# A two-layer adapter network on one core: the order of work inside a step, and who issues the gathers

## The reference, cut to what matters

```python
def layer(x, A, B, ids, W, b, experts_A, experts_B, router):
    c = einsum('bni,bri->bnr', x, B[ids])        # rank-16 coefficients
    v = einsum('bnr,bor->bno', c, A[ids])        # back to 1024 features
    y = v @ W.T + b                              # dense part
    z = einsum('bth,erh->bter', v, experts_A)    # 4 experts of rank 8
    alpha = softmax(v @ router.T (+ bias, log prior in layer 0))
    return x + y + 2 * sum_e alpha_e * (z_e @ experts_B_e.T)
```

## Time and profile before

| | us |
|---|---|
| median of 3 runs | 335.08 (334.63 to 335.91) |
| the profiled execution: its own time | 334.41 |
| the profiled execution: its span | 332.7 |
| PE busy in the span | 307.0 (92%) |
| DVE, ACT, POOL busy | 220.1, 186.4, 63.3 |
| from the issue of a load of x to its landing, median of 28 | 5.0 |

### The profile page before, as it was taken

How to read it: one execution, slowest core, us unless ns; L and a number is a source line. 1 busy time by engine, 2 the same in 40 slices (tenths; PEclk the granted TensorE clock), 3 DMA queues, 4 the chain that set the end, 5 groups by cost and what they waited for, 6 DMA issues and landing times.

```text
span 332.7 us, 6476 instructions
## 1 busy us (share of the span) xinstructions
PE 307.0 (92%) x2048; PEld 284.4 (85%) x2048; DVE 220.1 (66%) x476; ACT 186.4 (56%) x384; POOL 63.3 (19%) x58
## 2 busy tenths in 40 slices
PE   5994998799989998999979999999999999999894
PEld 4453998589978998999979999999999999899783
DVE  2156887686738766686658666777668676864556
ACT  1446976946546565755466465646575657461520
POOL 5600000620042103320143003320332024200000
PEclk9999899999999999999999999999999999999999
DMA  7999973006870388126840587037811783041006
GB/s 267 345 365 381 347 208 156 0 8 167 300 224 0 104 243 302 51 60 212 286 139 0 158 284 250 2 103 244 299 47 55 255 292 92 0 193 62 1 0 252
DMA packets 30773, 56.16 MB, mean 169 GB/s; under 512 B 3633, under 2 KB 20050, under 8 KB 30754
## 3 DMA queue, kind: packets, MB, share of 16 engines
q1 hardware_dynamic: 29666, 52.97, 48.3%
q0 software_dynamic: 1088, 2.97, 2.5%
HBM read 39.15 MB, written 16.78 MB: 168 GB/s over the span
## 4 chain that ended last, share of the span: by engine, by line
issue 41%; PE 20%; DMA 13%; POOL 12%; DVE 6%; ACT 3%; SPq 2%; POOLq 1%; DVEq 0%; ACTq 0%
POOL xs_lo L952 8%; DMA out<-xraw 6%; DMA xraw<-x_in 6%; PE ps_d L307 3%; PE ps_d L309 3%; PE ps_d L308 3%; POOL a1s_lo L952 2%; DVE xs_lo L740 2%; DVE xraw L942 2%; PE ps_d L545 1%; PE ps_p L307 1%; PE ps_d L547 1%; ACT res L574 1%; SPq L253 1%; SPq L251 1%
## 5 line engine op out<-in xcount | busy, mean ns | idle before, releaser
L952 POOL TENSOR_TENSOR xs_lo<-xraw,xs_hi 128x512 fp32r<-128x512 f32 x28 | 36.0, 1290 | 182.5 <-ACT xs_hi L574 182.4
L307 PE MATMUL ps_d<-w1s_hi,a1s_hi 128*128 128x384 f32 (+1 forms) x192 | 63.9, 333 | 0.0
L309 PE MATMUL ps_d<-w1s_hi,a1s_lo 128*128 128x384 f32 (+1 forms) x192 | 62.0, 323 | 0.0
L308 PE MATMUL ps_d<-w1s_lo,a1s_hi 128*128 128x384 f32 (+1 forms) x192 | 61.9, 322 | 0.0
L942 DVE SCALAR_TENSOR_TENSOR xraw<-ps_d,lp,xraw 128x512 f32<-128x512 f32 x60 | 43.6, 748 | 22.5 <-PE ps_d L547 22.5
L574 ACT ACTIVATE xs_hi<-xraw 128x512 fp32r<-128x512 f32 x60 | 36.0, 626 | 26.4 <-DMA xraw<-x_in 25.9
L307 PE MATMUL ps_p<-xs_hi,bst_hi 128*128 128x256 f32 x120 | 36.5, 304 | 6.2 <-DVE bst_lo L740 2.4
L308 PEld LDWEIGHTS ps_d<-w1s_lo,a1s_hi 128*128 128x128 f32 x192 | 36.2, 189 | 0.0
L307 PEld LDWEIGHTS ps_d<-w1s_hi,a1s_hi 128*128 128x128 f32 x192 | 36.1, 188 | 0.0
L309 PEld LDWEIGHTS ps_d<-w1s_hi,a1s_lo 128*128 128x128 f32 x192 | 36.1, 188 | 0.0
L308 PE MATMUL ps_p<-xs_lo,bst_hi 128*128 128x256 f32 x120 | 34.5, 288 | 0.0
(11 more groups left out here) (227 smaller groups left out, 702.9 us busy)
## 6 DMA issues: line engine op xcount, KB each, us to landing
out<-xraw SPq DMA_DIRECT2D x31, 512.0 KB, 3.5
xraw<-x_in SPq DMA_DIRECT2D x28, 512.0 KB, 5.0
w_plain<-w SPq DMA_DIRECT2D x16, 512.0 KB, 8.9
abraw<-ab_tab SPq DMA_DIRECT2D x64, 128.0 KB, 2.1
b0raw<-b_tab SPq DMA_DIRECT2D x64, 64.0 KB, 2.0
xraw<-x_in POOLq DMA_DIRECT2D x4, 512.0 KB, 11.0
a_plain<-a SPq DMA_DIRECT2D x1, 512.0 KB, 3.6
out<-xraw SPq DMA_DIRECT2D x2, 256.0 KB, 2.7
```

The costliest lines, as they stand in the source:

```text
L307: pe.matmul(acc, lh, rh, start=first, stop=False, skip_group_check=True)
L308: pe.matmul(acc, lh, rl, start=False, stop=False, skip_group_check=True)
L309: return pe.matmul(acc, ll, rh, start=False, stop=final, skip_group_check=True)
L952: return pool.tensor_tensor(dst, whole, high.bitcast(F32), ALU.subtract)
```

## The change

Four edits. PE's order within a step: `wide(0)` is cut behind its third chunk, so that `route(0)` comes earlier, and `wide(2)` as a whole stands behind `query()`. ACT and DVE do the softmax and the coefficients of layer 0 first, and the takings of `wide(0)` and the b parts of the next step behind them; two chunks of `split_x` that stood before the exponential go behind the b parts too. DVE's low parts `ht` and `he` go into the softmax, before its wait for the exponential. POOL issues the 16 gathers of a step instead of SP, with the ids read into registers at the head of its step.

```diff
--- before.py
+++ after.py
@@ -244,7 +244,7 @@
 
                 return tuple(zip(values(g * GROUP, GROUP, ADAPT0), values(g * GROUP + SEQS, GROUP, SEQS)))
 
-            def gather(picks, seqs, signal=gathered):
+            def gather(picks, seqs, signal):
 
                 for b in seqs:
                     n0, n1 = picks[b]
@@ -263,20 +263,12 @@
             gather(picks, range(HSEQ, GROUP), first_gathered[1])
             for k in range(KT):
                 sp.dma_start(w1raw[k], w1[k]).then_inc(w1_in[k], 16)
-            picks = pick(1)
-            sp.wait_ge(b_lo, 4)
-            sp.wait_ge(a_lo, 1)
-            gather(picks, range(GROUP))
             sp.wait_ge(x_used, 2 * CH)
             for i in range(CH):
                 load_x(1, 1, i)
 
             def body(g, par, last):
                 ahead = not (isinstance(g, int) and g >= STEPS - 2)
-                if ahead:
-                    picks = pick(g + 2)
-                    sp.wait_ge(a_lo, g + 2)
-                    gather(picks, range(GROUP))
                 for i in range(CH - 1 if last else CH):
                     sp.wait_ge(d_out, KT * g + KC * (i + 1))
                     sp.dma_start(out[bass.ds(g, 1), :, KC * i:KC * (i + 1), :]
@@ -458,7 +450,7 @@
                             pick_m0(k - 3, (ps_s, ps_z)[k - 3])
                 else:
                     after_step(pe, d_out, KT * g)
-                    wide(0)
+                    wide(0, range(3))
 
                 pe.wait_ge(h_sum, 2 * g + 2)
                 if first:
@@ -470,9 +462,11 @@
                 pe.wait_ge(c0_lo, g + 1)
                 after_step(pe, l_done, 2 * g)
                 route(0, f0x)
-                if not first:
-                    wide(1)
-                wide(2, range(KT // 2))
+                if first:
+                    wide(2, range(KT // 2))
+                else:
+                    wide(0, range(3, KT))
+                    wide(1, range(2))
                 pe.wait_ge(ht_lo, g + 1)
                 for n in range(2):
                     mm = pe.matmul(ps_h[:, n * P:(n + 1) * P], pick[:], ht[:, n, :], start=True, stop=True,
@@ -480,7 +474,10 @@
                 mm.then_inc(htx_done, 1)
                 pe.wait_ge(l_done, 2 * g + 1)
                 turn()
-                wide(2, range(KT // 2, 3 * KT // 4 if last else KT))
+                if first:
+                    wide(2, range(KT // 2, KT))
+                else:
+                    wide(1, range(2, KT))
 
                 def query():
 
@@ -496,8 +493,8 @@
                               skip_group_check=True).then_inc(q_done, 1)
 
                 query()
-                if last:
-                    wide(2, range(3 * KT // 4, KT))
+                if not first:
+                    wide(2)
                 if first:
                     pick_m0(2, ps_h)
                 banks = result_banks(last)
@@ -523,14 +520,14 @@
                 if first:
                     pick_m0(3, ps_s)
                 if last:
-                    start_results((0, 1, 2, 3, 4))
+                    start_results((0, 1, 2, 3))
                 else:
                     project(g + 1, 1)
                 pe.wait_ge(l_done, 2 * g + 2)
                 turn()
                 if last:
-                    from_layers(5)
-                    from_layers(6)
+                    for m in (4, 5, 6):
+                        from_layers(m)
                 else:
                     if first:
                         pe.wait_ge(m0x_ready, 8)
@@ -661,10 +658,6 @@
 
             def body(g, par, last):
                 first = isinstance(g, int) and g == 0
-                if not last and not first:
-                    act.wait_ge(h_done, g + 1)
-                    split_b(g + 1)
-
                 def wide_high(n):
                     cols, at = WIDE_PARTS[n]
                     width = min(cols.stop, D) - cols.start
@@ -685,28 +678,21 @@
                     act.wait_ge(sm_step, 9 * g + 4 * layer + 3)
                     act.activation(ex[:], lg[:], ACT.Exp).then_inc(exp_done, 1)
 
-                wide_high(0)
                 act.wait_ge(ht_done, g + 1)
                 copy(ht[:, 0, :], ps_t[:, 0:P]).then_inc(ht_hi, 1)
                 copy(he[0:LR, :], ps_t[0:LR, P:2 * P]).then_inc(ht_hi, 1)
-                if not last and not first:
-                    split_x(g + 1, 1 - par, 0, [0, 1])
                 softmax_exp(0)
-                wide_high(1)
                 act.wait_ge(htx_done, g + 1)
                 for half in range(2):
                     copy(htx[L0ROWS[half], half, :, :].rearrange("p a n -> p (a n)"), ps_h[L0ROWS[half], 0:2 * P]
                          ).then_inc(htx_ready, 1)
                 coef_high(0)
-                if first:
-                    split_b(g + 1, QUARTERS[0:2])
+                wide_high(0)
                 if not last:
-                    split_x(g + 1, 1 - par, 0, range(CH) if first else [2, 3])
-                wide_high(2)
-                if first:
-                    split_b(g + 1, QUARTERS[2:4])
+                    split_b(g + 1, QUARTERS[0:2] if first else QUARTERS)
                 if not last:
-                    split_x(g + 1, 1 - par, 1, [0])
+                    split_x(g + 1, 1 - par, 0)
+                wide_high(1)
                 act.wait_ge(c1_done, 2 * g + 1)
                 for half in range(2):
                     cols = slice(half * HALF, (half + 1) * HALF)
@@ -715,8 +701,11 @@
                     copy(cf[L1ROWS[half], 0, cols], cm[L1ROWS[half], cols]).then_inc(c1_hi, 1)
                 if first:
                     m0x_high(0, 2, ps_h)
+                wide_high(2)
+                if first:
+                    split_b(g + 1, QUARTERS[2:4])
                 if not last:
-                    split_x(g + 1, 1 - par, 1, range(1, CH))
+                    split_x(g + 1, 1 - par, 1)
                 softmax_exp(1)
                 if first:
                     m0x_high(0, 3, ps_s)
@@ -881,6 +867,10 @@
                     dve.tensor_tensor(lg[:], logits,
                                       mx.rearrange("p (j a) -> p j a", a=1).to_broadcast([P, TT, EXP]),
                                       ALU.subtract).then_inc(sm_step, 1)
+                    if layer == 0:
+                        dve.wait_ge(ht_hi, 2 * g + 2)
+                        low(ht[:, 1, :], ps_t[:, 0:P], ht[:, 0, :])
+                        low(he[ELO, :], ps_t[0:LR, P:2 * P], he[0:LR, :]).then_inc(ht_lo, 1)
                     if layer == 1 and not last:
                         split_second_x(g + 1, 1 - par, [3])
                     dve.wait_ge(exp_done, 2 * g + layer + 1)
@@ -899,15 +889,11 @@
                                       lg[:].rearrange("p j (e a) -> p j e a", a=1)
                                       .to_broadcast([P, TT, EXP, ER]), ALU.mult).then_inc(l_done, 1)
 
+                softmax(0)
+                coef_low(0)
+                if not last:
+                    split_b(g + 1, (0, 1) if first else range(4))
                 wide_low(0)
-                dve.wait_ge(ht_hi, 2 * g + 2)
-                low(ht[:, 1, :], ps_t[:, 0:P], ht[:, 0, :])
-                low(he[ELO, :], ps_t[0:LR, P:2 * P], he[0:LR, :]).then_inc(ht_lo, 1)
-                softmax(0)
-                wide_low(1)
-                coef_low(0)
-                if first:
-                    split_b(g + 1, (0, 1))
 
                 dve.wait_ge(q_done, g + 1)
                 for half in range(2):
@@ -922,6 +908,7 @@
                     dve.wait_ge(c1_hi, 2 * g + half + 1)
                     low(cf[L1ROWS[half], 1, cols], cm[L1ROWS[half], cols], cf[L1ROWS[half], 0, cols]
                         ).then_inc(c1_lo, 1)
+                wide_low(1)
                 if first:
                     split_b(g + 1, (2, 3))
                 if not last:
@@ -984,12 +971,39 @@
                 pool.dma_start(xraw[0][:, KC * i:KC * (i + 1), :], x_in[0, :, KC * i:KC * (i + 1), :]
                                ).then_inc(x0_in[i], 16)
 
+            def values(first, count, limit):
+
+                return nc.values_load_multi_w_load_instructions(
+                    ids[0:1, bass.ds(first, count)], (mybir.EngineType.Pool,), min_val=0, max_val=limit - 1)[1]
+
+            def pick(g):
+
+                return values(g * GROUP, GROUP, ADAPT0), values(g * GROUP + SEQS, GROUP, SEQS)
+
+            def gather(n0s, n1s):
+
+                for b, (n0, n1) in enumerate(zip(n0s, n1s)):
+                    pool.dma_start(b0raw[:, b, :],
+                                   b0_tab[bass.ds(n0, 1)].rearrange("a p n -> p (a n)")).then_inc(gathered, 16)
+                    pool.dma_start(abraw[:, b, :, :].rearrange("p a n -> p (a n)"),
+                                   ab1_tab[bass.ds(n1, 1)].rearrange("a p n -> p (a n)")).then_inc(gathered, 16)
+
             def body(g, par, last):
+                ahead = not (isinstance(g, int) and g >= STEPS - 2)
+                if ahead:
```

(12 more changed lines are left out.)

## The result

The changed kernel takes 337.48 us (median of 18 runs, 336.36 to 339.76), the kernel before 334.99 beside it: the ratio is 1.0091, 95% interval 1.0067 to 1.0116. It is slower by 0.9%, where 333.8 us, 0.4% less and no measurable change, was forecast; 337.48 lies in the range of 330.5 to 338.5, but on the other side of the kernel before.

A forecast was written before the change was run, and what follows sets the result against it. PE, busy 92% at full clock, bounds the kernel, so only its waits can change. Six steps -0.4, first step +1.2, last -2.1: -1.3 on the 332.7 us span, median 333.8 us, range 330.5 to 338.5.

The forecast's parts named there:

- Gathers to POOL: SP loses 9 us of issuing, x lands by T + 10 (T: first ps_h matmul); POOL's issues cost nothing.
- Layer 0 first: In each middle step lp is ready at T + 7.55, before turn() at T + 8.27; 6.2 us of waits go.
- b parts and x behind the coefficients: POOL starts x at T + 14.25, ends at 19.35; PE gets a new wait of 0.8 us in project.
- chunks of over 1.3 us: Sign of being wrong: POOL's chunks of x's low parts taking over 1.3 us, against 1.27 to 1.29 assumed.
- The layer-1 coefficients: Before route(1), DVE's second cf low part waits for POOL, then f1s: route(1) at about T + 20.45, step 25.35 us.
- cost POOL nothing: Claim that POOL's start on x in the first step, with DVE still at a b part, cost POOL nothing.
- The start at 58.50: POOL's start on x's low parts in the first step before the change, taken as evidence that overlap costs POOL nothing.
- The sum: Whole span: -0.4 for six steps, +1.2 first, -2.1 last, together -1.3 us; 333.1 profiled, 333.8 median.
- the lock goes both ways: Rival: POOL also stands during DVE's low parts, PE's last chunk 0.75 us later, 5 us in all, 339; chance 0.14.
- Step 0: First step: POOL starts 0.4 us later, route(1) 0.8, project(1, 1) 1.2; +1.2 us, near 31.0.
- The last step: Final step: PE's 2.1 us wait for layer-1 coefficients goes, a 0.3 softmax wait may come; together -2.1 us.
- a real gain: Rival: POOL's pace and DVE's order don't bind, route(1) at 19.5, steps 24.35; about 328 us, halfway 331; chance 0.34.

The follow-up runs named there:

- e1: Kernel before with only the 16 gathers of a step issued by POOL instead of SP, other order unchanged: 356.46 us, ratio 1.0557 to the kernel before.
- e9: Changed kernel, whole work, layer-1 coefficients kept in PSUM so DVE's subtraction for cf's low part has one SBUF input: 329.72 us, ratio 0.9876 to the kernel before.
- e13: Changed kernel with extra matmuls nobody reads ahead of chunks 2 and 3 of project(g+1, 0), from step 1 on: 336.78 us, ratio 1.0045 to the kernel before.
- e14: e9 with the first step alone in the order of before on ACT and DVE: 327.89 us, ratio 0.9782 to the kernel before.
- e4: Changed kernel, POOL subtracting only the first half of each chunk of x's low part, work left out: 327.63 us, ratio 0.975 to the kernel before.
- e5: Changed kernel with DVE writing zeros instead of subtracting for the layer-1 coefficients' low part: 327.88 us, ratio 0.9784 to the kernel before.
- e6: Changed kernel with ACT, from step 1 on, taking x chunks before and between the b parts, wide(0) behind: 359.98 us, ratio 1.0744 to the kernel before.
- e2: Changed kernel with its gathers given back to SP, so the new order alone: 341.31 us, ratio 1.0176 to the kernel before.

## Why the prediction went wrong, by its own steps

**Gathers to POOL: right, but its cover was the order.** The issues take 0.54 us and end at T + 0.2; ACT's wait for x falls from 25.9 to 3.1 us. What I had not priced is the landing (2.1 to 4.0 us in the median); the new order hides it, and e1 shows the 5.6% it costs without.

**Layer 0 first: right.** turn() starts at T + 8.34 (8.27 forecast), with no wait for lp.

**b parts and x behind the coefficients: the place right, the pace off.** POOL starts at T + 14.31 (14.25) and ends at T + 19.74 instead of 19.35. Its four chunks take 5.43 us instead of 5.1. The prediction had named chunks of over 1.3 us as a sign of being wrong; the next paragraph says where they come from.

**The layer-1 coefficients: the step that failed.** The prediction let DVE wait for POOL, and put the price for POOL at nothing ("cost POOL nothing"). The lock goes both ways. In step 2, one chunk at a time:

```profile
134.74 0.69 DVE L729 TENSOR_TENSOR bst_lo<-abraw,bst_hi 128x512 fp32r<-128x512 f32 x1
135.06 1.51 POOL L939 TENSOR_TENSOR xs_lo<-xraw,xs_hi 128x512 fp32r<-128x512 f32 x1 [14.09 <-ACT xs_hi L571]
...
136.54 1.30 POOL L939 TENSOR_TENSOR xs_lo<-xraw,xs_hi 128x512 fp32r<-128x512 f32 x1
...
139.03 1.46 POOL L939 TENSOR_TENSOR xs_lo<-xraw,xs_hi 128x512 fp32r<-128x512 f32 x1
```

The first chunk starts while DVE is still at the last low part of b, and the last has cf's low parts beside it; with the third, at 1.28, the two between them keep the forecast pace. In e9, where the collision with cf is gone, the last chunk takes 1.28 too, and the first still 1.52, which makes its 5.26. The start at 58.50, from which the prediction argued, had a low part of b on DVE beside it for only 0.20 us (it ends at 58.70), and its first chunk took 1.33. So POOL ends 0.39 us late. DVE's second low part of cf and f1s follow POOL as forecast, and route(1) starts at T + 20.87 instead of 20.45. From route(1) to the results I had taken 4.9 us, and it is 5.03, since DVE comes late to the second bank's x. Together a step at full clock takes 25.90 instead of 25.35: 0.55 x 6 = 3.3 us, 0.42 of each 0.55 ahead of route(1) and 0.13 behind it.

The whole collision with cf is worth more than this miss, 1.05 us a step by e9, 0.65 of it behind route(1) (4.38 instead of 5.03). The sum, through DVE's wait, had 0.50 of such a price (25.35 against e9's 24.85). The rival "the lock goes both ways" had the mechanism. It moved PE's last chunk by 0.75 us, where POOL's end moved by 0.39, and a step takes 25.90, just at the T + 25.9 from which I had let it decide.

**Step 0: right, but for the clock.** 31.0 forecast, 32.01 in the profile, 31.09 in e13, where its last stretch is at full clock. Against e14's 29.61 with the old order, that is 1.5 for the order; e13's still has the collision with cf in it.

**The last step: right.** T to the end of the program is 32.5 us against 34.9, 2.4 less (2.1 forecast).

**The sum.** At full clock the profiled execution would have taken 339.76 - 4 x 0.93 = 336.0, 2.9 over the forecast for the profile (333.1): +3.3 for the steps, +0.1 for step 0, -0.3 for the last, and -0.2 for what lies around them. With the 0.7 from profile to median that is 336.7; the measured median has 0.8 more. That 0.8 I put down to the low clock, which my sum had not at all: the mean clock is 0.983 over 18 runs against 0.987 in the later rounds of the kernel before. This last is argued, not shown.

**The rival "a real gain"** named the cure (cf's low parts out of POOL's way) and put it at 328 us. e4, e5 and e14 stand at 327.6 to 327.9, but that they meet this number is luck: it came from route(1) at T + 19.5 and steps of 24.35, e4 and e5 leave work out, and e14 has route(1) at T + 20.45, steps of 24.8 and its old step 0.

## What to carry to other kernels

When a re-ordering puts subtractions with two SBUF inputs on DVE and on POOL at the same time, price the collision on both of them, and then everything queued behind the one that waits; here 1.7 us on a DVE instruction pair came back as 1.05 us of every step. Before re-ordering again, see if one operand can stay in PSUM: that turned a 0.9% loss into a gain of 1.2%, and of 2.2% with step 0 left in its old order. A step that runs once, with other work in it than the loop's, should be ordered by itself.

## What the hardware showed that I had not expected

- Work of DVE and POOL that alternates, each with two inputs in SBUF, is slower on both: 0.69 us becomes 1.7 to 1.8 on DVE, 1.3 becomes 1.6 on POOL (e6). In the changed kernel a chunk of POOL that starts beside a low part of b on DVE takes 1.51 us instead of 1.28.
- The same DMA landed later when POOL issued it: 2.1 us in the median from SP, 4.0 in the changed kernel and 5.0 in e1. The Trainium skill ("DMA: Bandwidth & Descriptors", Issuing engines are not separate DMA queues) says that the issuing engine saves only the sequencer's time and the transfers interleave; here the 9 us of issuing were worth 0.8% (1.0091 against 1.0176 in e2), and the landing was no longer the same. What else was in flight differs too, as SP's stores no longer stand behind the gathers, so these runs don't show that the issuing engine is the cause.
- The granted clock is 0.62 in the mean, that is mostly the lower of its two levels (1.2 GHz), over a whole stretch of 4.45 us in which PE is busy throughout, in some steps and executions and not in others with the same waits ahead of it (0.23 and 0.44 us in step 2). Each such stretch costs 0.92 to 0.98 us. In e6, where PE waits up to 3.2 us for f1s, each of steps 1 to 6 has low-clock stretches, with a mean of 0.88 to 0.94 over the step.
